# A fused selective-scan and expert layer on one core: ten of sixteen state inflows of the first batch formed on TensorE by diagonal matrices, the first sum taken earlier, and constants, B/C and last weights loaded in other places

## The chip, the cores and the metric

One NeuronCore of a Trainium2 chip runs the whole program. The metric is the device time of one execution in microseconds (us). TensorE's clock has two levels, 1.2 and 2.4 GHz; the profile gives the granted clock of a stretch as a share of the higher one. VectorE, ScalarE, GpSimd and TensorE work side by side and meet at semaphores; SyncE issues nearly all DMAs.

## What is computed

Four batches of 1024 tokens, all in fp32. The first layer is a selective state space model:

```python
x  = einsum('ed,bld->bel', in_proj_w, ctx)              # 512 -> 1024 channels
u  = silu(causal_conv(x, conv_w, taps=4) + conv_b)
dt_lo, B, C = split(einsum('ke,bel->bkl', x_proj_w, u)) # 32, 16, 16 rows
delta = softplus(dt_proj_w @ dt_lo + dt_proj_b)
for t:                                                  # 16 states n per channel
    state[n] = state[n] * exp(delta[t] * A[n]) + delta[t] * u[t] * B[n, t]
    y[t] = sum_n state[n] * C[n, t]
x = x_in + (y + D * u) * silu(layernorm(x_in))
```

The second layer normalizes x, takes eight router logits per batch over all of its 1024 x 1024 values (weights of 33.5 MB, here "sw"), picks two of eight small experts per batch, adds their gated outputs, and multiplies by w3 with bias b3. The result is added to x.

## The kernel before

**Tiles and steps.** Channels lie on partitions: eight blocks of 128. The time axis is cut in two halves of 512. A step g (0 to 63) is one block of one half of one batch; 16 steps are a batch, 8 a half batch. Each step has eight slots (q = 0 to 7), and each slot handles one pair of the 16 states, n = 2q and 2q + 1. Beside a batch's scans, the plan (class Schedule, L60) places the work of the layer behind it: from batch 1 on, the expert layer of the batch before; in batch 0 only the statistics of the next batch's layer norm and half of its own logits. After the last step there is a tail with the last batch's logits, experts and w3 product.

**One pair.** ScalarE makes the decays dA = exp(delta * A[n]) (L1127, four buffers, so it runs four scans ahead). VectorE multiplies du by the broadcast row B[n] into one of two PSUM banks, M0 or M1 (times_b, L1338, the operation at L1343), and then runs the scan over 512 time points (L1370), which writes h. GpSimd saves the last state in the first half (L785) and multiplies the pair's h by C (L791). TensorE transposes the product onto the sum in PSUM bank YT (sum_pair, L849, the matmuls at L854): eight transposes of 128x128 against the identity. h has room for three pairs (RH = 3), so a scan of pair q waits for the sum of pair q - 3. VectorE's products for slot q + 1 stand at the end of slot q, after its two scans.

**Once per step.** du = delta * u is made by GpSimd at slot 4 of the step before (L748, du_s) and copied by ScalarE to PSUM in slot 7 (copy_du, L1080), after the last products of the step have read the old one. ScalarE makes D*u at slot 0 (L1115). In slot 2 VectorE multiplies the finished sum of the step before by the gate (L1287); TensorE then starts the new sum with D*u (L967) and pair 0. In slots 1 and 2 stand also the three convolution taps of a block ten steps ahead (L1218) and TensorE's projection to delta (L846); in slot 3 VectorE ends the softplus (L1248); in slot 4 TensorE turns z (L954); in slot 6 ScalarE takes silu of the gate and of u, loads tables (L1056, L1151), and TensorE does the input projection of a later block (L825).

**Rows of B and C.** After the last block of a half batch TensorE forms 64 rows (L837); ScalarE copies B and C to bcs, SyncE stores them in HBM (bc_scratch) and loads them back, each row broadcast over 128 partitions: Bb and Cb, 16 rows of 512 each, one DMA per pair for B and one for C (load_bc, L540). Later half batches reload the rows as the last step of the half before frees them.

**The start.** SyncE asks in turn for the context, the eight weight blocks of the first projections and, between them, eight rows of x for layer norm. ScalarE's queue issues eleven small constants (L1029) ahead of its own work: the last six belong to the expert layer (b1c and b2c twice, b3c, swb). TensorE waits once for all eleven (const_loaded) before its first x projection. Eight blocks are projected (L861), tapped, and rows taken for layer norm; two more blocks follow. SyncE waits for the tenth projection before it loads B and C, since rows 8 to 11 of Bb hold the second context until then.

**The tail.** The last logits need 32 tiles of 512 KB of sw. Nineteen buffers (ring_t) are free one after another: three of sww, four of w3h, eight in Cb, four in Bb. SyncE asks for them from the tail's slot 0 on (L669), the rest as TensorE has used a tile.

## Time and profile before

| | us |
|---|---|
| median of 3 runs | 2579.28 (2577.56 to 2580.72) |
| the profiled execution | 2580.0 |
| its span, first to last instruction | 2578.2 |
| VectorE busy | 2238.0 (87%) |
| TensorE busy | 1940.0 (75%), mean granted clock 0.858 |
| ScalarE busy | 1537.1 (60%) |
| GpSimd busy | 1446.6 (56%) |

The profile is of one execution. Busy time of an engine counts overlapping instructions once. The row of an operation names its line in the kernel, its engine (PE is TensorE, PEld its weight loads, DVE VectorE, ACT ScalarE, POOL GpSimd, SPq and ACTq the queues in which SyncE and ScalarE issue), what it writes and reads, and its shapes. A bracket behind a row gives the engine's idle time before it and what ended that time. A TensorE matmul of fp32 data shows as two records, a transpose as one.

### The profile page before, as it was taken

The numbers are of one execution on the slowest core, as the hardware profiler recorded it, in microseconds if no ns is written. First come the engines' busy times: TensorE is split into PE (matmuls) and PEld (weight loads), VectorE is DVE, ScalarE is ACT, GpSimd is POOL, SyncE is SP. The second block draws the span as 40 slices with busy tenths as digits, with TensorE's granted clock in tenths as the row PEclk, the third lists the DMA queues.
The fourth block names the chain that finished last, engine by engine and source line by source line (L and its number), as shares of the span: only waits on it lengthen the run. The fifth ranks groups of instructions, "written<-read, shape, count | busy, mean of one in ns | idle before, by whom it ended". The sixth has DMA issues, their size and how long they took to land.

```text
span 2578.2 us, 30156 instructions
## 1 busy us (share of the span) xinstructions
PE 1940.0 (75%) x9488; PEld 1093.3 (42%) x9488; DVE 2238.0 (87%) x2928; ACT 1537.1 (60%) x2221; POOL 1446.6 (56%) x990
## 2 busy tenths in 40 slices
PE   5565656666776898898675888799685797896799
PEld 2344444344443454454443455344453354453244
DVE  3899999999999899998999989998999999995210
ACT  1566556555667657854666757855576858852400
POOL 0477666666775556665775656565775666663000
PEclk8767776887887899998787999999787999997899
DMA  5411252545552364566452364466460274566511
GB/s 150 164 33 57 83 172 76 178 147 176 194 174 100 98 216 147 158 207 200 170 206 74 116 229 139 141 215 197 159 235 21 72 238 147 175 193 226 211 57 66
DMA packets 201617, 387.84 MB, mean 150 GB/s; under 512 B 31697, under 2 KB 97233, under 8 KB 201458
## 3 DMA queue, kind: packets, MB, share of 16 engines
q1 hardware_dynamic: 194992, 385.43, 44.8%
q10 hardware_dynamic: 6466, 0.48, 0.2%
q8 instruction: 76, 1.25, 0.2%
q14 instruction: 83, 0.68, 0.1%
HBM read 351.78 MB, written 34.08 MB: 150 GB/s over the span
## 4 chain that ended last, share of the span: by engine, by line
PE 32%; DVE 26%; issue 23%; ACT 9%; POOL 6%; DMA 2%; SPq 1%; DVEq 1%; ACTq 1%; POOLq 0%
DVE h L1370 12%; PE dense L1007 10%; PE dense L854 7%; DVE dense L1343 5%; POOL h L791 5%; PE dense L825 4%; ACT dA L1127 3%; DVE u L1218 3%; PE dense L837 2%; PE dense L928 1%; PE dense L938 1%; ACT L1084 1%; PE dense L846 1%; DVE szT L1287 1%; PE dense L861 1%
## 5 line engine op out<-in xcount | busy, mean ns | idle before, releaser
L791 POOL TENSOR_TENSOR h<-h,Cb 128x1024 f32<-128x1024 f32 x512 | 1208.5, 2360 | 456.3 <-DVE h L1370 432.7
L1127 ACT ACTIVATE dA<-delta,Av 128x512 f32<-128x512 f32 x1024 | 702.6, 717 | 519.9 <-DVE h L1370 517.4
L854 PE MATMUL dense<-ident,h 128*128 128x128 f32 x4096 | 643.3, 313 | 289.6 <-POOL h L791 287.5
L854 PEld LDWEIGHTS dense<-ident,h 128*128 128x128 f32 x4096 | 550.9, 162 | 465.5 <-POOL h L791 376.8
L1370 DVE TENSOR_TENSOR_SCAN h<-dA,state,dense 128x512 f32<-128x512 f32 x512 | 627.6, 1263 | 41.3 <-PE dense L854 22.4
L1343 DVE TENSOR_TENSOR dense<-dense,Bb 128x512 f32<-128x512 f32 x1024 | 652.9, 683 | 5.0 <-DMA Cb<-bc_scratch 2.9
L1370 DVE TENSOR_TENSOR_SCAN h<-dA,dense 128x512 f32<-128x512 f32 x512 | 597.3, 1202 | 17.6 <-ACT dA L1127 9.9
L1007 PE MATMUL dense<-w3h,xT 128*128 128x512 f32 x832 | 390.5, 603 | 0.0
L785 POOL COPY state<-h 128x2 f32<-128x2 f32 x256 | 48.0, 187 | 373.3 <-DVE h L1370 371.8
L846 PE MATMUL dense<-dtaug,dtw 33*128 33x512 f32 x128 | 103.0, 896 | 180.0 <-DVE u L1218 178.2
L825 PE MATMUL dense<-ctxs,win 128*128 128x512 f32 x432 | 224.4, 667 | 1.9 <-ACT dtw L1063 1.0
L1007 PEld LDWEIGHTS dense<-w3h,xT 128*128 128x128 f32 x832 | 149.1, 194 | 129.6 <-issue 129.6
L1218 DVE SCALAR_TENSOR_TENSOR u<-dense,cw,u 128x511 f32<-128x511 f32 (+2 forms) x192 | 140.3, 731 | 35.8 <-ACT u L1041 28.0
L1084 ACT ACT_TABLE_LOAD x113 | 145.0, 1283 | 2.0
L1329 DVE TENSOR_TENSOR res<-dense,res 128x512 f32<-128x512 f32 x64 | 43.8, 684 | 111.3 <-PE dense L1007 110.9
L825 PEld LDWEIGHTS dense<-ctxs,win 128*128 128x128 f32 x432 | 90.9, 221 | 111.4 <-issue 111.4
L986 PE MATMUL dense<-sww,row 128*32 128x256 f32 x1336 | 110.9, 418 | 14.3 <-ACT row L1160 14.3
L1080 ACT COPY dense<-du_s 128x512 f32<-128x512 f32 x64 | 37.6, 588 | 134.2 <-DVE dense L1343 134.2
L846 PEld LDWEIGHTS dense<-dtaug,dtw 33*128 33x128 f32 x128 | 25.6, 249 | 211.3 <-issue 211.3
L938 PE MATMUL dense<-hs,w2s 128*64 128x512 f32 x224 | 71.3, 707 | 41.4 <-ACT hs L1192 40.6
L748 POOL TENSOR_TENSOR du_s<-delta,u 128x512 f32<-128x512 f32 x64 | 81.6, 1275 | 5.7 <-DVE delta L1248 5.7
L778 POOL TENSOR_TENSOR xt<-szT,xt 128x512 f32<-128x512 f32 x64 | 81.7, 1277 | 3.0 <-DVE szT L1287 3.0
(141 smaller groups left out, 1846.0 us busy)
## 6 DMA issues: line engine op xcount, KB each, us to landing
sww<-in_sw SPq DMA_DIRECT2D x170, 512.0 KB, 4.4
Bb<-bc_scratch SPq DMA_DIRECT2D x64, 512.0 KB, 4.6
Cb<-bc_scratch SPq DMA_DIRECT2D x64, 512.0 KB, 5.8
w3h<-in_sw SPq DMA_DIRECT2D x56, 512.0 KB, 7.6
w3h<-in_w3T SPq DMA_DIRECT2D x52, 512.0 KB, 5.1
row<-x_scratch SPq DMA_DIRECT2D x42, 512.0 KB, 4.8
xz<-in_x SPq DMA_DIRECT2D x64, 256.0 KB, 5.0
xt<-in_x SPq DMA_DIRECT2D x64, 256.0 KB, 4.4
```

The source lines that it names most:

```text
L791: e.tensor_tensor(h[:, s:s + 2, :], h[:, s:s + 2, :], Cb[:, 2 * q:2 * q + 2, :], ALU.mult).then_inc(prod_done, 1)
L825: mm = e.matmul(dense[:, bank, :], win[:, par, k, :], ctxs[:, k, :], start=(k == 0), stop=(k == DK - 1))
L846: e.matmul(dense[:, S, :], dtw[0:DR + 1, j * P:(j + 1) * P], dtaug[:], start=True, stop=True) \
L854: mm = e.matmul(yT[:, k, :], h[:, 2 * (q % RH) + i, k * P:(k + 1) * P], ident[:], is_transpose=True, start=False, stop=(q == PAIRS - 1 and ...
L938: mm = e.matmul(dense[HD * i:HD * i + HD, bank, :], w2s[:], hs_of(b, hp)[:, i, :], start=True, stop=True)
L986: mm = e.matmul(dense[32 * n:32 * n + 32, F2, 0:32 * E], rows[:, lo:lo + 32], weights[:, :, 32 * n:32 * n + 32], start=first, stop=(k % TB ...
L1007: mm = e.matmul(dense[:, bank, :], xT_of(b, uu)[:, d, k * P:(k + 1) * P], w3[:, d, :], start=False, stop=(d == J - 1), skip_group_check=True)
L1084: e.preload_act_table_set("natural_log_exp_and_others")
L1127: e.activation(dst, delta[:, st % 2, :], ACT.Exp, scale=Av[:, j * N + n:j * N + n + 1]).then_inc(dA_done, 1)
L1218: i = e.scalar_tensor_tensor(out=u[:, G % UR, s:T], in0=dense[:, bank, 0:T - s], scalar=cw[:, j, k:k + 1], in1=u[:, G % UR, s:T], op0=ALU. ...
L1343: e.tensor_tensor(duB[:, n % 2, :], du[:], Bb[:, n, :], ALU.mult).then_inc(duB_done, 1)
L1370: e.tensor_tensor_scan(h[:, 2 * (q % RH) + n % 2, :], decay, inflow, state[:, j * N + n:j * N + n + 1] if th else 0.0, ALU.mult, ALU.add) \
```

## The change

In batch 0 alone, the pairs 1, 2, 4, 5 and 6 of each step (ten of sixteen states) get their product du*B from TensorE: du is transposed (turn_du, four transposes at slot 7), ScalarE copies it to SBUF (copy_duT), and each product is four matmuls of 128x128, du transposed by a diagonal matrix of B's values. VectorE makes the diagonals once per half batch (diagonal_b) from B's rows transposed on TensorE (turn_b) and puts them where the broadcast rows of B were; those rows are no longer loaded. Products go round three PSUM banks in place of two. On TensorE a product stands at the head of a slot (n = 2q + 3) and one after the planned work of the slot (n = 2q + 4). The D*u transposes and the sum of pair 0 (first_sum) move, in batch 0, from behind slot 2's planned work to the head of slot 2. VectorE keeps pairs 0, 3 and 7. Batches 1 to 3 keep all products on VectorE.

In the start, the six expert constants go from ScalarE's queue to SyncE's, behind the first inputs; the weight blocks are asked for two places ahead of the rows of x; and B and C of pairs 0 to 3 are asked for without the wait for the tenth projection. For the tail, four more buffers (in u) hold switch weights that are asked for in slots 0, 2, 4 and 6 of step 62. The removed names POOLED, VEC and pool_index stood for an empty set of states and changed nothing.

```diff
+PE_PAIRS = (1, 2, 4, 5, 6)
...
-RING_A, RING_B, RING_T = 8, 3, 19
+RING_A, RING_B, RING_U, RING_T = 8, 3, 4, 23
...
+def on_pe(g, n):
+
+    return g < STEPS and n // 2 in PE_PAIRS
+
+
+def product_bank(g, n):
+
+    return (F1, M0, M1)[(N * g + n) % 3] if g < STEPS else (M0, M1)[n % 2]
...
-        for i in range(RING_T):
-            self.add(b, 0 if i < RING_B + 4 else 5, "sw_load", TB + i // SWL, i % SWL)
+        for i in range(RING_U):
+            self.add(b - 1, 112 + 2 * i, "sw_ahead", i)
+        for i in range(RING_U, RING_T):
+            self.add(b, 0 if i < RING_U + RING_B + 4 else 5, "sw_load", TB + i // SWL, i % SWL)
...
-        ring_t = [*ring_b, *sw_tiles(w3h[:], 4), *sw_tiles(Cb[:], 8), *sw_tiles(Bb[:, 8:16, :], 4)]
+        ring_t = [*sw_tiles(u[:, 4:UR, :], 3), *sw_tiles(u[:, 0:2, :], 1), *ring_b, *sw_tiles(w3h[:], 4), *sw_tiles(Cb[:], 8), *sw_tiles(Bb[:, 8:16, :], 4)]
```

Loads and constants (SyncE, and ScalarE's list):

```diff
-        CONSTS = 11
+        CONSTS, FFN_CONSTS = 5, 6
...
+            return N * g + n - pe_index(g, n)
+
+        def bank_free(g, n):
+
+            return N * g + n - (2 if g < STEPS else 1)
+
+        def bc_value(c, q):
+
+            return 1 + sum(16 if on_pe(J * i, 2 * q) else 32 for i in range(c + 1))
...
-                for i, dst in ((0, Bb), (N, Cb)):
+                for i, dst in ((N, Cb),) if on_pe(J * c, 2 * q) else ((0, Bb), (N, Cb)):
...
-            for k in range(J):
-                if k:
+            for k in range(J + 2):
+                if 0 < k < J:
                     e.dma_start(first_win[k], w_inT[k]).then_inc(first_win_loaded[k], 16)
+                if k < 2:
+                    continue
+                k -= 2
                 e.dma_start(first_rows[k], x[0:1, k * P:(k + 1) * P, :].rearrange("o p d -> p (o d)")) \
                     .then_inc(first_row_loaded[k], 16)
...
             load_xz(0, 0, 0)
+            with nc.allow_non_contiguous_dma(reason="small weights, once"):
+                for dst, src in (
+                    (b1c[0:HD], b1.rearrange("e f -> f e")),
+                    (b1c[HD:P], b1.rearrange("e f -> f e")),
+                    (b2c[0:HD], b2.rearrange("e d -> d e")),
+                    (b2c[HD:P], b2.rearrange("e d -> d e")),
+                    (b3c[:], b3.rearrange("(j p) -> p j", p=P)),
+                    (swb[:], sw_b.partition_broadcast(P)),
+                ):
+                    e.dma_start(dst, src).then_inc(ffn_const_loaded, 16)
             e.wait_ge(xin_done, 1 + J + 1)
             load_ctx(0, 1)
             e.wait_ge(evac[S], 1 + FIRST_S)
             e.dma_start(bc_d[0], bcs).then_inc(bc_stored, 16)
             e.wait_ge(bc_stored, 1 + 16)
-            e.wait_ge(xin_done, 1 + 1 + AHEAD)
             for q in range(PAIRS):
+                if q == J // 2:
+                    e.wait_ge(xin_done, 1 + 1 + AHEAD)
                 e.wait_ge(first_row_read, 1 + q + 1)
                 load_bc(0, q)
...
+                    elif what == "sw_ahead":
+                        last = ALL - AHEAD + 2 * a[0] + 1
+                        e.wait_ge(uD_done, 1 + last + 1)
+                        e.wait_ge(du_s_done, 1 + last + 1)
+                        dst, done, _ = sw_tile(NB, TB, a[0])
+                        e.dma_start(dst, sw[TB * P:(TB + 1) * P, a[0]]).then_inc(done, 16)
...
+                        if b == NB:
+                            m -= RING_U
+                        ring = RING_B if k < TB else RING_A if b < NB else RING_T - RING_U
                         if m >= ring:
-                            e.wait_ge(sw_used, 1 + sw_index(b, k, i) - ring + 1)
+                            e.wait_ge(sw_used, 1 + sw_index(b, k, i) - (RING_T if b == NB else ring) + 1)
...
-                    (b1c[0:HD], b1.rearrange("e f -> f e")),
-                    (b1c[HD:P], b1.rearrange("e f -> f e")),
-                    (b2c[0:HD], b2.rearrange("e d -> d e")),
-                    (b2c[HD:P], b2.rearrange("e d -> d e")),
-                    (b3c[:], b3.rearrange("(j p) -> p j", p=P)),
-                    (swb[:], sw_b.partition_broadcast(P)),
```

GpSimd, TensorE and ScalarE:

```diff
                 e.wait_ge(du_done, 1 + g)
+                e.wait_ge(du_turned, 1 + min(g, STEPS))
...
+            def turn_du(g):
+
+                e.wait_ge(du_s_done, 1 + g + 1)
+                e.wait_ge(duT_done, 1 + g)
+                for k in range(TB):
+                    mm = e.transpose(dense[:, F0, k * P:(k + 1) * P], du_s[:, k * P:(k + 1) * P], ident[:])
+                mm.then_inc(du_turned, 1)
+
+            def turn_b(c, rows_copied):
+
+                e.wait_ge(evac[S], 1 + rows_copied)
+                for k in range(TB):
+                    mm = e.transpose(dense[:, F2, k * N:(k + 1) * N], bcs[0:N, k * P:(k + 1) * P],
+                                     ident[P - 2 * N:P - N, P - 2 * N:P - N])
+                mm.then_inc(b_turned, 1)
+
+            def times_b(g, n):
+
+                e.wait_ge(duT_done, 1 + g + 1)
+                if g % J == 0:
+                    e.wait_ge(diag_done, 1 + pe_index(1, 0) * (g // J) + pe_index(g, n) - pe_index(g, 0) + 1)
+                if N * g + n >= 3:
+                    e.wait_ge(h_done, 1 + bank_free(g, n))
+                for k in range(TB):
+                    mm = e.matmul(dense[:, product_bank(g, n), k * P:(k + 1) * P], duT[:, g % 2, k, :],
+                                  Bb[:, n, k * P:(k + 1) * P], start=True, stop=True)
+                mm.then_inc(duB_pe_done, 1)
+
+            def times_b_at(i):
+                g, n = divmod(i, N)
+                if on_pe(g, n):
+                    times_b(g, n)
...
+            turn_b(0, FIRST_S)
+            e.wait_ge(evac[F0], 1 + 2)
+            turn_du(0)
+            times_b_at(2)
+
+            def first_sum(g):
+
+                e.wait_ge(yg_done, 1 + g)
+                e.wait_ge(uD_done, 1 + g + 1)
+                for k in range(TB):
+                    e.matmul(yT[:, k, :], uD[:, k * P:(k + 1) * P], ident[:], is_transpose=True,
+                             start=(k == 0), stop=False, skip_group_check=True)
+                sum_pair(g, 0)
...
+                if b == 0:
+                    if q == 1 and j == J - 1 and g + 1 < STEPS:
+                        turn_b(c + 1, count(b, "x_proj", th) + 1)
+                    if q == 2:
+                        first_sum(g)
+                    times_b_at(N * g + 2 * q + 3)
...
+                if b == 0 and q != SLOTS - 1:
+                    times_b_at(N * g + 2 * q + 4)
+                if b == 0 and q == SLOTS - 1 and g + 1 < STEPS:
+                    turn_du(g + 1)
                 if late(b, t, 0):
                     sum_pair(g - 1, PAIRS - 1)
-                if b < NB:
-                    if q == 2:
-
-                        e.wait_ge(yg_done, 1 + g)
-                        e.wait_ge(uD_done, 1 + g + 1)
-                        for k in range(TB):
-                            e.matmul(yT[:, k, :], uD[:, k * P:(k + 1) * P], ident[:], is_transpose=True,
-                                     start=(k == 0), stop=False, skip_group_check=True)
-                        sum_pair(g, 0)
-                    if q >= 2:
-                        sum_pair(g, q - 1)
+                if b < NB and q == 2 and b:
+                    first_sum(g)
+                if b < NB and q >= 2:
+                    sum_pair(g, q - 1)
+                if b == 0 and q == SLOTS - 1:
+                    times_b_at(N * g + 2 * q + 4)
...
+            def copy_duT(g):
+
+                e.wait_ge(du_turned, 1 + g + 1)
+                if g >= 2:
+                    e.wait_ge(duB_pe_done, 1 + pe_index(g - 1, 0))
+                e.copy(duT[:, g % 2].rearrange("p k e -> p (k e)"), dense[:, F0, :]).then_inc(duT_done, 1)
...
+            copy_duT(0)
...
                     if q == SLOTS - 1 and g + 1 < ALL:
                         copy_du(g + 1)
+                        if g + 1 < STEPS:
+                            copy_duT(g + 1)
```

VectorE:

```diff
+            def diagonal_b(c, n):
+
+                e.wait_ge(b_turned, 1 + c + 1)
+                if c:
+                    e.wait_ge(duB_pe_done, 1 + pe_index(J * c - 1, n + 1))
+                e.tensor_tensor(Bb[:, n, :].rearrange("p (k t) -> p k t", k=TB), ident[:].unsqueeze(1).broadcast_to([P, TB, P]),
+                                dense[:, F2, 0:TB * N].rearrange("p (k n) -> p k n", k=TB)[:, :, n:n + 1]
+                                .broadcast_to([P, TB, P]), ALU.mult).then_inc(diag_done, 1)
+
+            for n in range(N):
+                if on_pe(0, n):
+                    diagonal_b(0, n)
...
+                    if N * g + n >= 3:
+                        e.wait_ge(h_done, 1 + bank_free(g, n))
+                    e.tensor_tensor(dense[:, product_bank(g, n), :], du[:], Bb[:, n, :], ALU.mult).then_inc(duB_done, 1)
 
                 if g == 0 and q == 0:
-                    e.wait_ge(bc_loaded[0], 1 + 32)
+                    e.wait_ge(bc_loaded[0], bc_value(0, 0))
+                    e.wait_ge(evac[F1], 1 + 2)
                     for n in (0, 1):
-                        if n in VEC:
-                            times_b(0, n)
+                        times_b(0, n)
...
+                    if on_pe(g, n):
+                        e.wait_ge(duB_pe_done, 1 + pe_index(g, n) + 1)
                     else:
                         e.wait_ge(duB_done, 1 + vec_index(g, n) + 1)
...
-                    e.tensor_tensor_scan(h[:, 2 * (q % RH) + n % 2, :], decay, inflow,
+                    e.tensor_tensor_scan(h[:, 2 * (q % RH) + n % 2, :], dA[:, (N * g + n) % RA, :], dense[:, product_bank(g, n), :],
...
+                    if j == 0 and not on_pe(g, 2 * q + 2):
+                        e.wait_ge(bc_loaded[q + 1], bc_value(c, q + 1))
                     for n in (2 * q + 2, 2 * q + 3):
-                        if n in VEC:
+                        if not on_pe(g, n):
                             times_b(g, n)
                 elif g + 1 < ALL:
                     if j == J - 1:
-                        e.wait_ge(bc_loaded[0], 1 + 32 * (c + 2))
+                        e.wait_ge(bc_loaded[0], bc_value(c + 1, 0))
                     for n in (0, 1):
-                        if n in VEC:
-                            times_b(g + 1, n)
+                        times_b(g + 1, n)
+                if j == J - 1 and g + 1 < STEPS and q and on_pe(g + 1, 2 * (q - 1)):
+                    for n in (2 * q - 2, 2 * q - 1):
+                        diagonal_b(c + 1, n)
...
                 e.wait_ge(lg_done, 1 + b)
+                e.wait_ge(ffn_const_loaded, 1 + 16 * FFN_CONSTS)
```

## Rows read from the trace of the kernel before

**Rows 1.** Table of stages; each engine's busy us and count, TensorE clock, DMA share, GB/s.

```profile
90.00:610.00 520.00, 327.46 (x1556) 215.56 (x1557) 508.35 (x632) 307.78 (x460) 347.15 (x232) 0.75 0.35 116
...
1100.00:1200.00 100.00, 96.38 (x486) 49.37 (x482) 89.56 (x110) 50.50 (x76) 56.63 (x33) 1.00 0.59 192
```

**Rows 2.** Timeline of GpSimd, du of steps 1 and 16: start us, us, operation.

```profile
111.60 1.27 POOL L748 TENSOR_TENSOR du_s<-delta,u 128x512 f32<-128x512 f32 x1
...
609.62 1.28 POOL L748 TENSOR_TENSOR du_s<-delta,u 128x512 f32<-128x512 f32 x1
```

**Rows 3.** Timeline of VectorE, one slot of the first step.

```profile
99.02 2.32 DVE L1370 TENSOR_TENSOR_SCAN h<-dA,dense 128x512 f32<-128x512 f32 x2
101.26 1.27 DVE L1343 TENSOR_TENSOR dense<-dense,Bb 128x512 f32<-128x512 f32 x2
102.44 2.32 DVE L1370 TENSOR_TENSOR_SCAN h<-dA,dense 128x512 f32<-128x512 f32 x2
```

**Rows 4.** Waits, 110 to 610 us: total us, times, longest.

```profile
PEld dense L854 <- POOL h L791: 120.1, 64, 4.7
POOL h L791 <- DVE h L1370: 89.6, 51, 4.7
```

**Rows 5.** Timeline of TensorE: transposes at full clock; weight loads of the ones matmul.

```profile
2297.57 1.91 PE L854 MATMUL dense<-ident,h 128*128 128x128 f32 x16
...
751.88 0.53 PEld L901 LDWEIGHTS dense<-lgr,ones 128*128 128x128 f32 x4
```

**Rows 6.** Timeline, slots 6 and 7 of the first step and the next step's first scans.

```profile
113.46 4.41 PE L825 MATMUL dense<-ctxs,win 128*128 128x512 f32 x8
...
117.01 0.59 ACT L1080 COPY dense<-du_s 128x512 f32<-128x512 f32 x1 [1.77 <-DVE dense L1343]
...
120.25 2.32 DVE L1370 TENSOR_TENSOR_SCAN h<-dA,dense 128x512 f32<-128x512 f32 x2
```

**Rows 7.** Timeline of GpSimd, starts of two slots of the first half batch.

```profile
112.93 0.19 POOL L785 COPY state<-h 128x2 f32<-128x2 f32 x1
...
115.79 0.19 POOL L785 COPY state<-h 128x2 f32<-128x2 f32 x1 [0.17 <-DVE h L1370]
```

**Rows 8.** Timeline of the start: ScalarE's queue of constants; VectorE's first taps.

```profile
14.81 2.85 ACTq L1029 DMA_DIRECT2D b1c<-in_b  x2
...
23.54 7.81 ACTq L1029 DMA_DIRECT2D swb<-in_sw_b  x1
...
33.69 2.32 DVE L1218 SCALAR_TENSOR_TENSOR u<-dense,cw,u 128x511 f32<-128x511 f32 x3 [21.55 <-ACT u L1041]
```

**Rows 9.** Waits for constants in the start: timeline (wait in brackets), then waits in total.

```profile
20.70 0.16 POOL L722 MEMSET cw<- 128x72 f32 x1 [10.01 <-DMA cb<-in_conv_b]
...
PE dense L837 <- DMA swb<-in_sw_b: 11.9, 1, 11.9
```

**Rows 10.** Timeline of the start: first projections; VectorE's taps of blocks 6 and 7.

```profile
16.98 13.49 PE L861 MATMUL dense<-ctxs,Bb 128*128 128x512 f32 x24 [16.98 <-DMA Bb<-in_w_inT]
...
64.06 2.31 DVE L1218 SCALAR_TENSOR_TENSOR u<-dense,cw,u 128x511 f32<-128x511 f32 x3 [0.62 <-ACT u L1041]
...
68.69 2.31 DVE L1218 SCALAR_TENSOR_TENSOR u<-dense,cw,u 128x511 f32<-128x511 f32 x3 [0.62 <-ACT u L1041]
```

**Rows 11.** SyncE's wait before the B/C loads; last early taps and first products, timeline.

```profile
SPq L570 <- PE dense L861: 6.2, 1, 6.2
...
84.00 2.31 DVE L1218 SCALAR_TENSOR_TENSOR u<-dense,cw,u 128x511 f32<-128x511 f32 x3 [3.92 <-ACT u L1050]
...
89.20 1.30 DVE L1343 TENSOR_TENSOR dense<-dense,Bb 128x512 f32<-128x512 f32 x2 [2.88 <-DMA Cb<-bc_scratch]
```

**Rows 12.** The end: table of stages in two stretches; a piece of the chain.

```profile
2300.00:2310.00 10.00, 10.00 (x61) 5.75 (x60) 9.97 (x13) 6.56 (x9) 7.29 (x5) 1.00 0.54 152
...
2370.00:2380.00 10.00, 7.72 (x92) 2.94 (x84) 0.21 (x2) 3.02 (x4) 0.74 (x2) 0.84 1.02 408
...
2390.49 16.69 DMA Cb<-in_sw
```

More of the change, by code:

```diff
@@ L49, in conv_slot @@
     return 2 if st % J == J - 1 else 1
-def pooled(n):
-    return n % 2 == 1 and n // 2 in POOLED
-VEC = [n for n in range(N) if not pooled(n)]
+def on_pe(g, n):
+    return g < STEPS and n // 2 in PE_PAIRS
+def product_bank(g, n):
+    return (F1, M0, M1)[(N * g + n) % 3] if g < STEPS else (M0, M1)[n % 2]
 class Schedule:
@@ L298, in build @@
         du_s = sb("du_s", [P, T])
-        duB_s = sb("duB_s", [P, 2, T])
+        duT = sb("duT", [P, 2, TB, P])
         h = sb("h", [P, 2 * RH, T])
@@ L400, in build @@
         du_done = sem("du_done")
-        duB_s_done = sem("duB_s_done")
+        du_turned = sem("du_turned")
+        duT_done = sem("duT_done")
+        b_turned = sem("b_turned")
+        diag_done = sem("diag_done")
+        duB_pe_done = sem("duB_pe_done")
         dA_done = sem("dA_done")
@@ L462, in chunk_block, with pe_index @@
             return G // STEPS, G // J % TH, G % J
+        def pe_index(g, n):
+            return 2 * len(PE_PAIRS) * min(g, STEPS) + sum(on_pe(g, m) for m in range(n))
         def vec_index(g, n):
-            return NV * g + sum(m < n for m in VEC)
-        def pool_index(g, n):
-            return len(POOLED) * g + sum(pooled(m) for m in range(n))
+            return N * g + n - pe_index(g, n)
[3 more added lines that the diff above has]
+            return 1 + sum(16 if on_pe(J * i, 2 * q) else 32 for i in range(c + 1))
         def f_index(b, k):
@@ L649, in slot @@
                         m = SWL * (k % TB) + i
-                        ring = RING_B if k < TB else RING_A if b < NB else RING_T
+                        if b == NB:
+                            m -= RING_U
+                        ring = RING_B if k < TB else RING_A if b < NB else RING_T - RING_U
                         if m >= ring:
-                            e.wait_ge(sw_used, 1 + sw_index(b, k, i) - ring + 1)
+                            e.wait_ge(sw_used, 1 + sw_index(b, k, i) - (RING_T if b == NB else ring) + 1)
                         elif k < TB:
@@ L766, in _ @@
             du_of(0, 1 + FIRST_S + 1)
-            for q in (0, 1):
-                if q in POOLED:
-                    times_b(0, q)
             def slot(b, t):
@@ L996, in slot @@
                         if part == 0:
+                            if b == 1 and uu == 0 and dh == 0 and k == 0:
+                                e.wait_ge(ffn_const_loaded, 1 + 16 * FFN_CONSTS)
                             if dh == 0 and k == 0:
```

49 lines of the change are left out of this document (9 added, 40 removed).

## The prediction

> **What bounds the kernel now.** I read the table of stages first. In the first batch's stretch, 90 to 610 us, VectorE is busy 508.35 of 520 us, TensorE 327.46 at a mean granted clock of 0.75, GpSimd 347.15 [rows 1]. The reader should see one full engine and two that rest a third of the time. The stretch from 1100 us on is the opposite: TensorE 96.38 of 100 us at clock 1.00 and VectorE down to 89.56. A busy TensorE is given the full clock here, and when it fills up it takes time from VectorE. Next, the step's length: du is made once per step, and 15 steps lie between the second and the seventeenth du, (609.62 - 111.60) / 15 = 33.2 us [rows 2]. Then one slot in the timeline: two scans, then two products for the next slot, 102.44 - 99.02 = 3.42 us; the scans take 2.24 of it (99.02 to 101.26), the products 1.18 [rows 3]. Last the waits of this stretch: GpSimd waits 89.6 us for scans, TensorE's weight loads 120.1 us for GpSimd, and nobody long for a product [rows 4]. So each microsecond taken off VectorE here is worth up to one, until GpSimd or TensorE is full.
>
> **Products moved.** Five of eight pairs per step leave VectorE: 5 x 1.18 = 5.9 us per step, 16 steps: -94.4 us. VectorE now builds ten diagonals ident*B per half batch, each a product-sized operation (0.59 us, half of 1.18): the second ten in step 7, +5.9 us; the first ten stand in the start, below. VectorE's step becomes 33.2 - 5.9 + 0.4 = 27.7 us.
>
> **TensorE's side.** A moved product is four 128x128 fp32 matmuls of 128 columns, which the trace lacks. Near rows: sixteen transposes at full clock take 1.91 us, start to start about 0.11. The ones matmul (8 columns, full 128x128 weights, two passes each) loads its four weight sets in 0.53 us, about 0.113 per pass [rows 5]. If streaming hides behind the next load, a product is 8 x 0.113 = 0.9 us; if load and stream follow one another, 8 x (0.113 + 0.107) = 1.75, taking a transpose's 0.11 as a pass's streaming. I take 0.9, because the load row is the nearest (same weights, same two passes) and the projections' loads hide. Ten products and du's four transposes (0.45) are 9.5 us per step. The present work is 327.46 x 0.75 / 15.7 steps (520 / 33.2) = 15.7 us per step at full clock, so 25.2 in all: under VectorE's 27.7, but 84% of a 30 us step.
>
> The Trainium skill ("TensorE: Matmul & The Clock Gate", Terms) says that fp32 transpose mode on trn2 is four times faster than a plain fp32 matmul. By it, four transposes at 0.11 would make a product 4 x 4 x 0.11 = 1.76 us, not 0.9. No row settles it for 128 columns.
>
> **What takes some of it back.** (1) *The du chain.* ScalarE's copy of du transposed stands in the last slot, before the next step's D*u and first decays. Now the projection starts just as slot 6 begins and takes 4.41 us, GpSimd-fed sums follow, ScalarE copies du at 117.01, and the next step's first scan is at 120.25 [rows 6]. In the change TensorE reaches turn_du only after that projection, sum 5 (0.9) and its own 0.45: 5.8 us after slot 6 starts; the copy adds 0.6, D*u and a decay 0.7 each: 7.8. VectorE wants the decay after its 3.42 us slots 6 and 7, at 6.8. Slot 5 is 1.2 us shorter now, while the work that holds the projection back (ScalarE's gate and table loads) is not; I count half of that. About 1.6 us late; bounds 0 and 3. The queue behind the wait is ScalarE's: D*u and all decays of the next step. (2) *GpSimd.* In the first half batch a slot costs it 115.79 - 112.93 = 2.86 us [rows 7], above the 2.24 that VectorE needs in a slot without products. Its three-pair ring covers two such slots, not three (pairs 4, 5, 6). (3) *Queueing on TensorE*: first_sum waits at the head of slot 2 for the gating, and product 8, sum 1 and soon product 9 stand behind it. I put (2) and (3) at 0.7 us per step; bounds zero (lags fall into the slots with statistics or taps) and 3 us. So 27.7 + 2.3 = 30.0 us per step, 3.2 less than now: **-51 us** over 16 steps (94.4 - 5.9 - 37).
>
> **The start.** ScalarE issues its constants until 31.35: the six expert constants from 14.81, the last alone 7.81 us [rows 8]. Only then comes ScalarE's first tap, and VectorE's first at 33.69, 2.3 later. And TensorE waits 11.9 us (until 42.3) for the same last constant before it projects block 3; the wait names swb, though the work needs xpw. Afterwards ScalarE is bound only by cb, for which GpSimd waited 10.0 us, till 20.7 [rows 9]. First taps then at about 23.0, 10.7 earlier. The three first projections end at 16.98 + 13.49 = 30.5; block 3 can follow at once instead of after 42.3, if the five small constants have landed. Blocks come every 68.69 - 64.06 = 4.63 us [rows 10], three more such gaps before; so block 3's taps stood at 50.2, 8 us after the wait ended with a half-clocked TensorE; I take 6 after 30.5, hence 36.5, and block 7's taps at 55.0 in place of 68.69: 14 us earlier. Bounds: 10.7 if constants or input rows, which now follow two weight loads later, are late; 16 if VectorE alone paces. Moving six DMAs to SyncE costs its queue up to 16.5 us from 31.35, that is till 48; its next wait is for block 7's projection, which ends just before those taps, about 54: hidden. If that cover went, the second context load and all behind it (B/C store, loads) would be late by the excess.
>
> The B/C loads waited 6.2 us on SyncE for the last early projection, and VectorE 2.88 us for B and C (its products at 89.20, after taps starting at 84.00) [rows 11]. Half the loads no longer wait for it, and B/C come early enough; in that gap VectorE now makes ten diagonals, 5.9 us, 3.0 more than the wait. Start: -14 + 3 = **-11 us**. Five B loads of each half batch go too, at no gain: they lie beside VectorE's work.
>
> **The tail.** In the 2370s the DMA engines are full (share 1.02, 408 GB/s), and the chain waits on the last switch weights from 2390.49 to 2407.2 [rows 12]. Four tiles of 512 KB, asked for in the last step but one, where the share is 0.54, take 2.1 MB / 408 GB/s = **-5.1 us** out. Bounds 0 and 8 (with a longer ring, TensorE gates fewer loads). Nothing else waits for them: their buffers, u of finished steps, are free.
>
> **Sum.** -51 - 11 - 5 = -67 us. The profiled execution took 2580.0 us, span 2578.2 and 1.8 around it, 0.7 above the median of 2579.28. 2580.0 - 67 = 2513.0; as a median 2512.3.
>
> **Rivals.**
> *A. VectorE still binds.* TensorE's full clock and the statistics absorb all lags; step 27.7. For it: VectorE at 98% now, sums of all others below. Against: the 1100 us stretch, where VectorE drops to 89.56. Time: 94.4 - 5.9 + 11 + 5 = -105: 2475. Chance 0.14.
> *B. TensorE or the hand-over eats the whole gain.* Products cost about 1.3 us, midway between the two prices, TensorE's step 29.2 at full clock, and with waits 33: nothing in the batch, start and tail stay: 2580 - 16 = 2564. Chance 0.12.
> *C. Slower: a pass loads and streams in turn.* A product costs 1.75 us on TensorE, in every one of ten places per step: 15.7 + 17.5 + 0.45 = 33.7 at full clock, 35.4 at clock 0.95 (near the 1.00 of the full stretch), 2.2 above today's 33.2: +35 - 16 = +19: 2599. It decides from about 1.6 us per product on. For it: transposes' 0.11 could already be load plus stream. Against: the 0.113 row and hidden loads elsewhere. Chance 0.08. The factor of four in the Trainium skill ("TensorE: Matmul & The Clock Gate", Terms) would give nearly the same price.
> *D. The start moves nothing*, since the small constants land at 40 anyway: 2524, inside the forecast's own range.
> The forecast with its spread has 0.66.
>
> **How the numbers follow.** Likeliest 2512. Range: low 2478, near A; high 2558, between forecast and B; beyond lie half of B, all of C, a little of A. A measurement of this kernel tells 0.2% (5 us) from no change. Faster by more: forecast, A, B, 0.89; within: 0.03, between B and C; slower: 0.08, C.
>
> **What would show it.** First tap near 23 us, first scan near 79; steps of about 30 us with VectorE near 92% busy, TensorE's clock 0.9 or more, mean gaps before the first scan of a step ended by ScalarE's decay; products at 0.9 us per four. Wrong would be: scans waiting for TensorE's products on every slot (B, C), clock still at 0.75, or VectorE at 98% with 28 us steps (A).

## The result, and the profile after

The changed kernel takes 2555.16 us in the median of four runs (2554.08 to 2556.93); four runs of the kernel before gave 2578.91. The ratio is 0.9907, 95% interval 0.9893 to 0.9922: faster by 24 us where 67 were forecast, inside the range and near its upper end. The profiled execution took 2556.93 us, span 2555.1, 23.1 less than before.

The table of stages shows where it was not won. First the changed kernel: the stretch that rows 1 show of before, the full stretch of a later batch, and the sixteen steps from the second du to the eighteenth.

```profile
90.00:610.00 520.00, 420.49 (x2886) 327.82 (x2884) 430.38 (x492) 317.96 (x482) 351.32 (x233) 0.95 0.34 108
1100.00:1200.00 100.00, 86.15 (x401) 45.34 (x400) 88.61 (x107) 51.59 (x80) 56.82 (x34) 0.94 0.65 210
96.56:625.85 529.29, 423.01 (x2869) 327.99 (x2868) 439.95 (x505) 322.21 (x489) 357.13 (x238) 0.94 0.34 108
```

The same view of the kernel before, for the same sixteen steps:

```profile
111.60:644.99 533.39, 339.11 (x1600) 222.43 (x1600) 520.97 (x648) 315.89 (x474) 357.92 (x239) 0.75 0.35 112
```

VectorE, the third pair of numbers, has 439.95 us of work in place of 520.97: 81 us less. But the sixteen steps take 529.29 in place of 533.39, only 4.1 less. VectorE rested 12.4 us before and rests 89.3 now. TensorE has neither become full nor kept a low clock: 423 of 529 us, at 0.94.

The start is where the forecast put it. Timeline of the changed kernel, VectorE: first taps, taps of block 7, diagonals, first products and first scans [rows 8, 10, 11]:

```profile
26.51 2.32 DVE L1288 SCALAR_TENSOR_TENSOR u<-dense,cw,u 128x511 f32<-128x511 f32 x3 [13.84 <-ACT u L1106]
...
55.27 2.31 DVE L1288 SCALAR_TENSOR_TENSOR u<-dense,cw,u 128x511 f32<-128x511 f32 x3
...
72.82 6.06 DVE L1352 TENSOR_TENSOR Bb<-ident,dense 128x512 f32<-128x512 f32 x10
78.79 1.29 DVE L1426 TENSOR_TENSOR dense<-dense,Bb 128x512 f32<-128x512 f32 x2
79.99 2.32 DVE L1450 TENSOR_TENSOR_SCAN h<-dA,dense 128x512 f32<-128x512 f32 x2
```

The first scan comes at 79.99, before at 90.41. The second du (GpSimd's timeline) is 15.0 us earlier than in rows 2, since step 0 also is 4.6 us shorter:

```profile
96.56 1.27 POOL L785 TENSOR_TENSOR du_s<-delta,u 128x512 f32<-128x512 f32 x1
```

Cut at starts of du, the gain of 23.1 us is 15.0 up to the second du, 4.1 in the next sixteen steps, 0.7 in the 46 steps to the last du, and 3.3 behind it. The waits of the changed kernel from 98 to 575 us, which answer to rows 4, show what VectorE rests for (total us, times, longest):

```profile
ACT duT L1152 <- PE dense L872: 46.1, 15, 7.1
DVE h L1450 <- PE dense L905: 44.1, 30, 7.2
DVE h L1450 <- ACT dA L1195: 30.8, 14, 7.3
```

L1450 are the scans, L905 the sums of the pairs, L872 the transposes of du. Scans now wait 44.1 us for sums and 30.8 us for decays; in the same stretch of the kernel before, the first wait was absent and the second 4.6 us. Not one of the long ones is for a product (L891): those make 0.6 us together. Where in the step it happens, the timeline of an ordinary step shows (changed kernel, the change from step 3 to step 4):

```profile
189.27 2.32 DVE L1450 TENSOR_TENSOR_SCAN h<-dA,dense 128x512 f32<-128x512 f32 x2
...
194.16 2.33 DVE L1450 TENSOR_TENSOR_SCAN h<-dA,dense 128x512 f32<-128x512 f32 x2 [1.38 <-ACT dA L1195]
...
195.53 2.24 PE L891 MATMUL dense<-Bb,duT 128*128 128x128 f32 x16 [1.21 <-DVE h L1450]
...
196.82 2.36 POOL L812 TENSOR_TENSOR h<-h,Cb 128x1024 f32<-128x1024 f32 x1
...
197.60 1.04 PE L905 MATMUL dense<-ident,h 128*128 128x128 f32 x8
198.78 1.22 DVE L1450 TENSOR_TENSOR_SCAN h<-dA,dense 128x512 f32<-128x512 f32 x1 [1.64 <-PE dense L905]
```

The scans of pair 0 start at 194.16, those of pair 1 at 198.78. h is indexed by the pair's number within the step, modulo three. That ring is whole inside a step only: pairs 7 and 1 have the same place, as have pairs 6 and 0. So a step's second pair waits for the sum of the last pair of the step before, two pairs back and not three. On TensorE that sum (197.60) stands behind two products that themselves wait for VectorE's scans to free a bank (195.53, with 1.21 us of waiting). Before, nothing stood there.

It is worst at the border of steps 6 and 7, just before the half batch's last step (changed kernel, timeline):

```profile
283.27 3.65 PE L855 MATMUL dense<-u,xpw 128*64 128x512 f32 x8
...
286.85 0.66 PE L872 MATMUL dense<-ident,du_s 128*128 128x128 f32 x4
...
287.54 0.59 ACT L1152 COPY duT<-dense 128x512 f32<-128x512 f32 x1 [6.24 <-PE dense L872]
288.03 0.57 ACT L1127 COPY dtaug<-dense 32x512 f32<-32x512 f32 x1
...
290.75 2.33 DVE L1450 TENSOR_TENSOR_SCAN h<-dA,dense 128x512 f32<-128x512 f32 x2 [5.03 <-ACT dA L1195]
...
293.08 5.29 PE L843 MATMUL dense<-ctxs,win 128*128 128x512 f32 x8
...
299.11 1.04 PE L905 MATMUL dense<-ident,h 128*128 128x128 f32 x8
...
300.28 2.33 DVE L1450 TENSOR_TENSOR_SCAN h<-dA,dense 128x512 f32<-128x512 f32 x2 [7.20 <-PE dense L905]
```

Two chains follow one another. x_proj stands before du's transposes, ScalarE's copy waits 6.24 us for these, and two copies of x_proj's rows (from 288.03), D*u and the decays stand behind it: VectorE rests 5.03 us. Then the input projection (5.29 us) and a product stand before the last sum: VectorE rests 7.20 us. TensorE was busy 0.88 us from 290 to 293, and its mean granted clock was 1.00 there and 0.72 from 293 to 299, the projection's stretch; at clock 1.00, from 187.31, the same projection took 3.60 us. So 1.7 us of the second wait are the low clock, granted after TensorE's rest; in e5_all_three, after a like rest (from 272.50), it took 3.60.

### The profile page after: what moved, and what is told of

The parts are those of the page before. It is cut to its first block, busy times and chain, and to the rows that moved or that the text cites. A ratio compares the mean times of both kernels' runs of the same rounds, so it can differ in the third digit from the quotient of the medians.

```text
span 2555.1 us, 32784 instructions
## 1 busy us (share of the span) xinstructions
PE 2032.3 (80%) x10840; PEld 1210.5 (47%) x10840; DVE 2157.7 (84%) x2788; ACT 1543.7 (60%) x2237; POOL 1444.5 (57%) x990
## 4 chain that ended last, share of the span: by engine, by line
PE 29%; DVE 18%; issue 15%; ACT 8%; POOL 5%; DMA 1%; SPq 0%; DVEq 0%; POOLq 0%; ACTq 0%
PE dense L1078 11%; DVE h L1450 8%; PE dense L905 6%; POOL h L812 4%; PE dense L843 4%; DVE dense L1426 3%; ACT dA L1195 2%; DVE u L1288 2%; PE dense L855 1%; ACT L1156 1%; PE dense L1008 1%; PE dense L998 1%; PE dense L1055 1%; ACT hs L1262 1%; PE dense L864 1%
## 5 line engine op out<-in xcount | busy, mean ns | idle before, releaser
L1195 ACT ACTIVATE dA<-delta,Av 128x512 f32<-128x512 f32 x1024 | 700.6, 717 | 473.5 <-DVE h L1450 471.3
L905 PE MATMUL dense<-ident,h 128*128 128x128 f32 x4096 | 603.2, 298 | 179.4 <-POOL h L812 178.1
L1450 DVE TENSOR_TENSOR_SCAN h<-dA,state,dense 128x512 f32<-128x512 f32 x512 | 628.0, 1265 | 80.0 <-PE dense L905 44.7
L905 PEld LDWEIGHTS dense<-ident,h 128*128 128x128 f32 x4096 | 519.0, 155 | 329.9 <-POOL h L812 244.2
L1450 DVE TENSOR_TENSOR_SCAN h<-dA,dense 128x512 f32<-128x512 f32 x512 | 597.3, 1204 | 46.7 <-PE dense L905 28.6
L1426 DVE TENSOR_TENSOR dense<-dense,Bb 128x512 f32<-128x512 f32 x864 | 551.2, 684 | 1.6
L891 PE MATMUL dense<-Bb,duT 128*128 128x128 f32 x1280 | 186.0, 292 | 77.3 <-DVE h L1450 72.7
L891 PEld LDWEIGHTS dense<-Bb,duT 128*128 128x128 f32 x1280 | 164.1, 201 | 111.6 <-issue 109.5
L843 PE MATMUL dense<-ctxs,win 128*128 128x512 f32 x432 | 210.6, 633 | 1.2 <-ACT dtw L1128 0.7
L864 PE MATMUL dense<-dtaug,dtw 33*128 33x512 f32 x128 | 91.6, 803 | 112.0 <-DVE u L1288 110.2
L843 PEld LDWEIGHTS dense<-ctxs,win 128*128 128x128 f32 x432 | 84.6, 205 | 101.7 <-issue 101.7
```

The source lines that it names most:

```text
L843: mm = e.matmul(dense[:, bank, :], win[:, par, k, :], ctxs[:, k, :], start=(k == 0), stop=(k == DK - 1))
L864: e.matmul(dense[:, S, :], dtw[0:DR + 1, j * P:(j + 1) * P], dtaug[:], start=True, stop=True) \
L891: mm = e.matmul(dense[:, product_bank(g, n), k * P:(k + 1) * P], duT[:, g % 2, k, :], Bb[:, n, k * P:(k + 1) * P], start=True, stop=True)
L905: mm = e.matmul(yT[:, k, :], h[:, 2 * (q % RH) + i, k * P:(k + 1) * P], ident[:], is_transpose=True, start=False, stop=(q == PAIRS - 1 and ...
L1195: e.activation(dA[:, i % RA, :], delta[:, st % 2, :], ACT.Exp, scale=Av[:, j * N + n:j * N + n + 1]).then_inc(dA_done, 1)
L1426: e.tensor_tensor(dense[:, product_bank(g, n), :], du[:], Bb[:, n, :], ALU.mult).then_inc(duB_done, 1)
```

## The experiments

H is the theory above: VectorE's step became as short as forecast, and waits between steps took the gain: the ring broken at the step's border, the last sum behind two products, and du's transposes late. The rival is that TensorE's products, or its load as such, set the pace. Lengths of steps below are the distances between starts of du on GpSimd (the 16 steps from the second du on; each one profiled execution). du stands at slot 4 of the step before, so "step 7" in the table runs from slot 4 of step 6 to slot 4 of step 7 and holds the border shown above; "rest" is their sum less VectorE's busy time in them.

| kernel | median us | ratio to before, 95% | steps 1 to 3 | 7 | 15 | 16 steps | VectorE busy | rest |
|---|---|---|---|---|---|---|---|---|
| before | 2578.91 | | 30.6 30.6 30.6 | 38.4 | 36.3 | 533.4 | 521.0 | 12.4 |
| changed | 2555.16 | 0.9907 [0.9893, 0.9922] | 30.7 29.5 29.0 | 46.7 | 43.2 | 529.3 | 440.0 | 89.3 |
| e2_last_sum_first | 2531.91 | 0.9813 [0.9796, 0.9829] | 27.7 27.4 27.2 | 45.4 | 40.8 | 509.3 | 440.3 | 69.0 |
| e3_turn_early | 2555.69 | 0.9916 [0.9894, 0.9938] | 30.5 28.4 27.9 | 46.7 | 43.7 | 528.7 | 440.4 | 88.3 |
| e4_ring | 2512.01 | 0.9738 [0.9722, 0.9755] | 26.7 26.5 26.5 | 45.5 | 40.8 | 497.0 | 438.5 | 58.5 |
| e5_all_three | 2489.40 | 0.9647 [0.9628, 0.9666] | 25.0 25.1 25.1 | 41.8 | 40.2 | 476.8 | 437.5 | 39.2 |
| e10_split_behind_decays | 2485.87 | 0.9635 [0.9619, 0.9651] | 25.0 25.1 25.0 | 40.2 | 38.5 | 471.3 | 437.7 | 33.6 |
| e11_three_pairs | 2521.95 | 0.9776 [0.9759, 0.9792] | 28.2 29.7 28.3 | 41.3 | 39.7 | 512.6 | 472.8 | 39.8 |
| e12_six_pairs | 2498.14 | 0.9673 [0.9656, 0.9691] | 25.3 25.3 25.3 | 42.1 | 40.0 | 476.7 | 422.6 | 54.0 |

**Start and tail without the products.** All products back on VectorE, no transposes or diagonals:

```diff
-PE_PAIRS = (1, 2, 4, 5, 6)
+PE_PAIRS = ()
...
-                if b == 0 and q == SLOTS - 1 and g + 1 < STEPS:
-                    turn_du(g + 1)
```

> The changed kernel with no pair on TensorE: its start, its constants and its tail, the old products everywhere. Both theories agree on the start; what it separates is how the 24 us divide. If the moved products brought almost nothing (theory H: what VectorE gave up came back as hand-over waits), this kernel alone takes about 2561 us (2558 to 2565): first scan near 75 us, 15 earlier than before, as there are no diagonals, and 3 us in the tail. If the products brought most of it, it takes 2570 or more. The steps of the first batch keep 33.2 us on average.

Measured: 2569.95 us, 0.9962 [0.9948, 0.9976]: 9 us slower than expected. The first scan was at 73.53, so the start held; the batch lost it again. The waits of this kernel, 98 to 575 us, name the place (L945 are the D*u transposes of the first sum):

```profile
PEld dense L945 <- DVE szT L1358: 99.9, 14, 9.1
PE dense L945 <- DVE szT L1358: 94.2, 14, 8.9
```

At the head of slot 2 TensorE waits about 7 us a step for the gating, with all its work of that slot behind it. In the changed kernel the same weight loads wait 26.1 us in all, 1.7 a step. The next kernel is the same with the first sum in its old place:

```diff
-                    if q == 2:
-                        first_sum(g)
...
-                if b < NB and q == 2 and b:
+                if b < NB and q == 2:
```

> Start, constants and tail of the change alone, with the old place of the first sum too. The run with the new place had du of step 1 16.9 us earlier than before and du of step 16 only 6.3 earlier, so the new place seems to cost the old products 0.7 us per step, because the projection to delta stands behind the wait for the gate. If so, this kernel takes 2559 us (2556 to 2562). If the loss comes from elsewhere (the third bank, the wait order), it stays at 2567 to 2572.

Measured: 2559.54 us, 0.9912 [0.9896, 0.9929]. So start and tail alone are worth 22 us, nearly all that the whole change gave (by estimate some 16 with the ten diagonals in the start, 6 us, which these two kernels don't make). In its profiled execution 17.5 us are won up to the second du and 6.7 behind the last one, and 3.2 are lost between. The first sum's new place costs 10 where TensorE makes no products.

**The first sum's old place, with the products on TensorE.** The edit just shown, now on the changed kernel:

> The changed kernel with D*u's transposes and the sum of pair 0 back behind slot 2's planned work and product 8. Theory H (order on TensorE decides): the sum of pair 0 comes 2 us later, pair 3 waits for it, ordinary steps grow by about 1 us: 2570 us (2563 to 2578). Rival: what first_sum gains for pair 3 it takes from the projection to delta behind it, so the place is indifferent here: 2552 to 2558.

Measured: 2595.44 us, 1.0051 [1.0034, 1.0068]; the sign as expected, but 25 us more. Scans wait 72.0 us for sums (98 to 575 us) in place of 44.1. The slot's product waits for a free bank and holds sum 0 back, and pair 3 needs sum 0's place in h. Timeline of this kernel, one step:

```profile
151.26 3.55 PE L905 MATMUL dense<-ident,h 128*128 128x128 f32 x16
153.31 2.33 DVE L1448 TENSOR_TENSOR_SCAN h<-dA,dense 128x512 f32<-128x512 f32 x2 [3.70 <-PE dense L905]
```

With products on TensorE the new place is thus worth 40 us (2595.4 to 2555.2), without them it costs 10.

**The constants.** The six expert constants back in ScalarE's queue, and all else as changed:

```diff
-        CONSTS, FFN_CONSTS = 5, 6
+        CONSTS = 11
```

> The changed kernel with the six expert constants asked for in ScalarE's queue again, as before the change; everything else as changed. The first taps came 7.2 us earlier and the first scan 10.4 us earlier in the changed kernel; if that queue held the start, the time goes back by 10 to 15 us: about 2568 (2565 to 2571). The rival, that the other edits of the start carry the gain: 2555 to 2558.

Measured: 2569.19 us, 0.9955 [0.9939, 0.9972], 14 us back; first taps at 33.94, first scan at 93.25. So the place of these six constants held the start. Both of their effects come back, ScalarE's later first operation (31.8 us in place of 24.3) and TensorE's wait of 12.4 us for the last constant; the run doesn't tell them apart.

**The three waits, one at a time.** First the last sum ahead of the slot's planned work and second product:

```diff
                     times_b_at(N * g + 2 * q + 3)
+                    if late(b, t, 0):
+                        sum_pair(g - 1, PAIRS - 1)
```

> The changed kernel, but in the first batch the sum of the last pair of a step stands on TensorE right behind the head product of the next slot 0, ahead of that slot's projection and second product. Theory H (order of hand-overs): steps 7 and 15 lose the 7.2 and 5.5 us that the scan of pair 1 waited for this sum behind a projection, ordinary steps lose 0.5 of their 1.6: about 2538 us (2533 to 2545). Theory T (TensorE's amount of work binds): the same instructions in another order, 2553 to 2557.

Measured: 2531.91 us, 0.9813 [0.9796, 0.9829], 23 us less than the changed kernel and 6 less than expected; 20 of them lie in the sixteen steps. Scans wait 16.7 us for sums in place of 44.1 (waits of this kernel, 98 to 560 us):

```profile
DVE h L1452 <- PE dense L905: 16.7, 26, 2.3
```

Then du's transposes ahead of slot 6's planned work instead of in slot 7:

```diff
+                    if q == 6 and g + 1 < STEPS:
+                        turn_du(g + 1)
```

> The changed kernel, but du is transposed at the head of slot 6, ahead of the projection, instead of in slot 7. Theory H: ScalarE's 46 us of waiting for the transposed du go, and with them VectorE's 31 us of waiting for decays, some of which turns into waits for sums: about 2537 us (2530 to 2545). Theory T: 2553 to 2557, as TensorE has the same work.

Measured: 2555.69 us, 0.9916 [0.9894, 0.9938]: a miss, no gain at all. The waits of this kernel, from 98 to 560 us, say why:

```profile
DVE h L1450 <- PE dense L905: 51.7, 41, 7.2
...
DVE h L1450 <- ACT dA L1195: 12.0, 3, 6.7
```

The wait for decays fell from 30.8 to 12.0 us, and that for sums rose, up to 575 us from 44.1 to 57.2. In the change to step 4 the scan of pair 0 now waits 1.10 us for a sum (it was 1.38 for the decay), and pair 1 waits 1.64 us as before: what came last was taken away, and another wait ended nearly as late. At the border of steps 6 and 7 the scan of pair 0 still waits 4.39 us for the decay, for ScalarE's copy of x_proj's rows waits for x_proj (5.57 us) ahead of it, and pair 1 still waits 7.18 us for its sum. The granted clock over the sixteen steps was 0.91 in place of 0.94; whether that hid a small gain was not tested.

Then the ring, counted over all pairs of all steps, so that it has three places everywhere:

```diff
-                    s = 2 * (q % RH)
+                    s = 2 * ((PAIRS * g + q) % RH)
...
-                        e.wait_ge(prod_summed, 1 + PAIRS + PAIRS * g + (q - RH + 1 if q >= RH else min(q - 1, 0)))
+                        e.wait_ge(prod_summed, 1 + PAIRS + PAIRS * g + q - RH + 1)
```

> The changed kernel, but h's three pair buffers go round without a break (pair index of the whole program modulo 3, and each scan waits for the sum three pairs back). Before, pair 7 and the next step's pair 1 share a buffer, so across a step the ring is two deep. Theory H: most of VectorE's 44 us of waiting for sums in the first batch goes, except behind the projections of steps 7 and 15: about 2538 us (2530 to 2547); later batches gain a few us too. Theory T: 2552 to 2557. A third theory, that GpSimd's rate binds: no more than 2 us either.

Measured: 2512.01 us, 43 us less than the changed kernel, 26 more than expected. Waits for sums fall from 44.1 to 7.1 us (98 to 560 us):

```profile
DVE h L1450 <- PE dense L905: 7.1, 14, 1.0
```

Its profiled execution, the fastest of its four, is 49 us below the changed kernel's: 32 in the sixteen steps (529.3 to 497.0 us) and 18 in the 46 steps behind them. GpSimd's rate, a third theory named in the expectation, would have left no more than 2. What the ring is worth in later batches the same edit on the kernel before shows by itself:

> The kernel before with the unbroken ring alone. In its first batch VectorE is 98% busy, so nothing is to be had there; later batches gained 16 us from the ring in the run with the change. Theory H: 2562 us (2558 to 2568), all of it after the first batch. Rival: the ring was already holding the first batch back before the change: 2550 or less.

Measured: 2565.26 us, 0.9939 [0.9922, 0.9955]. Its sixteen steps stay at 534 us, as before, and the 46 steps after them take 1644.1 us in place of 1662.9. The broken ring cost nothing in the first batch as long as VectorE was full, and 32 us once TensorE made products. All three edits together:

> The changed kernel with the three edits together: unbroken ring, last sum behind the head product, du transposed at slot 6. With the ring alone ordinary steps take 26.5 us, while step 7 still takes 45.5 and step 15 40.8, with 7.3 us of waiting for decays behind the late du copy and a sum behind a projection. Theory H: those two steps lose 8 to 12 us each, ordinary ones 0.5: about 2488 us (2480 to 2495). Rival: VectorE's diagonals and the softplus chain fill steps 7 and 15 and the ring had taken all else: 2505 to 2512.

Measured: 2489.40 us, 66 us less than the changed kernel, as expected. With the early sum and the early transposes the steps fall by another 20 us beside the ring; the wait for decays falls from 20.5 to 13.9 us. Which of the two edits brings how much was not tried. Table of stages and waits (98 to 560 us) of this kernel:

```profile
96.69:573.44 476.75, 410.38 (x2870) 321.06 (x2868) 437.53 (x505) 322.43 (x489) 356.95 (x238) 0.96 0.38 120
...
256.36:298.20 41.84, 32.52 (x173) 23.02 (x172) 30.91 (x40) 20.26 (x33) 22.61 (x20) 0.91 0.37 116
497.91:538.08 40.17, 34.14 (x222) 22.75 (x220) 26.12 (x27) 20.97 (x34) 22.21 (x15) 0.97 0.51 160
96.69:171.81 75.12, 68.88 (x501) 57.43 (x500) 74.18 (x82) 60.14 (x95) 67.80 (x56) 1.00 0.14 42
```

```profile
DVE h L1452 <- ACT dA L1197: 13.9, 4, 6.7
DVE h L1452 <- PE dense L905: 6.5, 15, 0.8
```

The last row are steps 1 to 3: VectorE works 74.18 of 75.12 us, so there it binds again. Steps 7 and 15 (second and third row) hold 25 of the 39 us that it rests.

**What binds then.** Three pairs, and six, in place of five on TensorE, each with the three edits:

```diff
-PE_PAIRS = (1, 2, 4, 5, 6)
+PE_PAIRS = (1, 4, 5)
```

> e5_all_three with TensorE making three of the sixteen du*B pairs' products a half step instead of five. If VectorE binds the steps once the waits are gone, the two products given back cost 2 x 1.18 x 16 = 37.8 us less the second diagonals that are saved: about 2522 (2510 to 2527). The rival, that TensorE's queue binds: no change or a gain, 2490 or less.

Measured: 2521.95 us. VectorE has 35 us more work, and the steps take 36 more.

> e5_all_three with six pairs' products on TensorE instead of five. If VectorE still binds: 1.18 x 16 = 19 us less, with a diagonal more about -16: 2474 (2470 to 2480). The rival, TensorE binds by then, since its work was 25 us of a 25 to 27 us step already: 2489 or more.

Measured: 2498.14 us. VectorE has 15 us less work and the sixteen steps take as long as with five (476.7); ordinary ones 25.3 in place of 25.0. Table of stages of this kernel, an early stretch:

```profile
100.00:200.00 100.00, 95.30 (x705) 81.17 (x704) 93.48 (x102) 77.55 (x123) 88.39 (x71) 1.00 0.16 47
```

TensorE is at 95 of 100 us at full clock (e5_all_three: 90), VectorE down to 93 (98.6). H is shown for three to five pairs, where the steps follow VectorE's work. At six they no longer do, and VectorE's wait for delta, which ScalarE makes from a TensorE projection, is 19.0 us in place of 6.7 (98 to 575 us). That fits the rival, but no kernel with six pairs takes load off TensorE to show it. Five is the best of the three numbers tried. That the median is 9 us above e5_all_three lies outside the sixteen steps: 3.4 before them and 6.5 in the 46 steps behind, less 1.1 after the last du. No kernel separates that.

**ScalarE's copy at the half batch's end.** In e5_all_three steps 7 and 15 still take 41.8 and 40.2 us, and the copy of x_proj's rows waits 6.40 us ahead of the decays. It was put behind them:

```diff
-                if b < NB and late(b, t, 0) and st % J == J - 1 and c + 1 < NB * TH:
-                    split_rows(c + 1)
...
+                    if late(b, t, 0) and st % J == J - 1 and c + 1 < NB * TH:
+                        split_rows(c + 1)
```

> e5_all_three with ScalarE's two copies that turn x_proj's rows into the delta input (split_rows) put behind the two decays of slot 0, in every batch. In e5's step 15 that copy waits 6.40 us for the second half of x_proj, and the decay that VectorE's scan waits 6.67 us for stands behind it. If a wait at the head of ScalarE's queue is what makes the two heavy steps 42 and 40 us long, each loses about 6 us, and the steps of later batches that carry an x_proj about 3 us each: about 2465 (2460 to 2478). The rival: these steps are long because VectorE and TensorE have more work in them (the diagonals, the softplus chain), and the copy's wait only shows it: then 2485 to 2490, and the heavy steps stay above 39 us.

Measured: 2485.87 us, and its interval overlaps e5_all_three's. The two steps lost 1.6 us each, not 6: a miss. Timeline of this kernel, step 15:

```profile
508.04 1.28 DVE L1452 TENSOR_TENSOR_SCAN h<-dA,state,dense 128x512 f32<-128x512 f32 x1 [3.53 <-ACT dA L1195]
...
515.50 0.75 DVE L1290 SCALAR_TENSOR_TENSOR u<-dense,cw,u 128x511 f32<-128x511 f32 x1 [4.03 <-ACT u L1117]
...
526.67 0.69 DVE L1320 SCALAR_TENSOR_TENSOR delta<-dense,delta 128x512 f32<-128x512 f32 x1 [3.21 <-ACT delta L1141]
```

The wait for the decay shrank from 6.67 to 3.53 us, and VectorE rests for other things of the new half batch: the taps' first term, and delta. What of this chain can be shortened was not tried. It is the fastest kernel found, 3.65% [3.49, 3.81] below before, and not told apart from e5_all_three.

## Why the prediction came out as it did

**The products' price and TensorE's load came as forecast.** In the changed kernel a product and the sum behind it start 0.89 us apart (timeline):

```profile
276.81 1.06 PE L891 MATMUL dense<-Bb,duT 128*128 128x128 f32 x8
...
277.70 1.04 PE L905 MATMUL dense<-ident,h 128*128 128x128 f32 x8
```

That is the 0.9 taken. By the factor of four that the Trainium skill ("TensorE: Matmul & The Clock Gate", Terms) gives for fp32 in transpose mode, the prediction's estimate was 1.76 us; the measurement says otherwise, and it decides. TensorE's work is 423.01 x 0.94 / 16 = 24.9 us a step (25.2 forecast). Rival C falls: no product is waited for (0.6 us in all). Of rival B the price of 1.3 us falls, but its other half, that the hand-over eats the whole gain, is nearly what happened: steps of 33 us, and 2555 us lies far nearer to B's 2564 than to the forecast's 2512.

**VectorE's work was right to a tenth.** 439.95 / 16 = 27.5 us a step, 27.7 forecast. It gave up 81 us where the forecast has 94.4 - 5.9 = 88.5; part of the difference is that the sixteen steps counted here end in the second batch.

**The step that failed is the hand-over, the term "2.3 us per step", sized 1.6 for the du chain and 0.7 for GpSimd and TensorE's queue.** The sixteen steps take 33.1 us each, so it measured 33.1 - 27.5 = 5.6 us. It takes the ring as three pairs deep everywhere ("Its three-pair ring covers two such slots, not three", said of GpSimd). At the step's border the ring has two places, and the wait line that says so (the min(q - 1, 0) of e4's diff) stood in the code. The prediction asked who waits for a product and how late du comes, and named the queue behind first_sum, but did not ask what stands ahead of the last sum of a step, and which scan needs that sum's place. With the ring as it had supposed, the kernel takes 2512.0 us, the predicted number. This agreement is partly luck: its sixteen steps take 497.0 / 16 = 31.1 us each, not 30.0, and 18 us of its profiled gain lie in later batches, which the forecast left alone. Only the three edits together bring the step to 476.8 / 16 = 29.8 us, with a hand-over of 2.5 us, most of it in the two heavy steps.

**An average hid the heavy steps.** The forecast spread VectorE's work evenly. Steps 7 and 15 were 38.4 and 36.3 us before and became 46.7 and 43.2: at their borders stand x_proj and the input projection behind it, and step 7 holds six of the ten diagonals. The other fourteen steps won 19 us together, and these two gave 15 back.

**The du chain** was real (30.8 us of waits, 1.9 a step, 1.6 forecast) but its edit alone was worth nothing: e3_turn_early.

**The start** was right to a few us: first scan 79.99 (79 forecast), block 7's taps 55.27 (55.0), though the first taps came at 26.51, not 23.0. **The tail** gave 3.3 us where 5.1 was taken, but no kernel tests it alone: from the last du to the end the kernels with the new tail take 263.6 to 268.3 us and e7_ring_before, with the old one, 268.8 (before: 270.3). By experiment start and tail are worth 22 us without the diagonals, by estimate 16 with them, as in the forecast.

**Rival A** (VectorE binds, 28 us steps) did not come: VectorE is busy 83% of the sixteen steps.

## What to carry to other kernels

When work leaves a full engine, price the moved work, but then walk every queue that it enters and ask for each instruction behind it which buffer its end sets free and who takes that buffer next; a ring that is indexed within a step is shorter at the step's border than its depth says. Do this for the heaviest step, not for the mean one. Taking away the wait that comes last can show nothing when another ends nearly as late (0 us for du's early transposes), so a null result says what one edit is worth beside the others as they stand, and no more.

## What the runs showed that was not expected

A place in a queue changed its sign with its neighbours: the first sum at the head of slot 2 costs 10 us with products on VectorE and saves 40 with them on TensorE.

The times of some kernels lie in two groups: e7_ring_before gave 2559.8 and 2562.1, then 2568.5 and 2568.7 us; e12_six_pairs 2489.9 once and 2497.8 to 2498.7 three times; e3_turn_early 2554.9 to 2555.9 three times and 2565.4 once; e5_all_three 2487.6 to 2489.9 three times and 2496.7 once; the changed kernel's four lie within 2.9. The profiled execution of e7_ring_before was its lowest, so the 18.9 us in later batches above is that run's (by medians the edit is worth 16), and the 6.5 us that e12_six_pairs loses in later batches may be of this kind. What makes the groups stays open.
